# Moving the weight splits of the paged attention to other places inside an item

## The reference

```python
# L1_cond2, per sequence: 32 query heads, 8 key/value heads of 128 channels
q = einsum('bsd,ed->bse', x, Wq); k = einsum('bsd,ed->bse', x, Wk); v = einsum('bsd,ed->bse', x, Wv)
q, k = rope(rmsnorm(q)), rope(rmsnorm(k))
k_all = concat([k_cache[block_table], k]); v_all = concat([v_cache[block_table], v])   # 512 cached + 128 own keys
probs = softmax(where(valid, q @ k_all^T * SCALE, -1e30))
o = probs @ v_all
h = einsum('bse,de->bsd', o, Wo)
# L1_ffn: layernorm, int8-like fake-quantised linear, gelu, another such linear; added to x
```

## Time and profile before

| | us |
|---|---|
| median of 3 runs | 2129.42 (2124.53 to 2130.46) |
| the profiled execution: its own time | 2129.42 |
| the profiled execution: its span | 2127.6 |
| busy in the span: PE, PEld | 2030.9, 1714.6 |
| busy in the span: DVE, ACT, POOL | 1538.7, 1333.8, 812.6 |
| items of the paged attention | from 972.86 to the end of the span |

### The profile page before, as it was taken

One profiled execution on the slowest core, in us unless ns is written; L12 is line 12 of the kernel. 1 busy time (PEld: TensorE's weight loads), 2 busy tenths in 40 slices (PEclk: granted clock), 3 DMA queues, 4 the chain that ended last, 5 costly groups with the idle time before them and its releaser, 6 DMA issues.

```text
span 2127.6 us, 35433 instructions
## 1 busy us (share of the span) xinstructions
PE 2030.9 (95%) x12241; PEld 1714.6 (81%) x12264; DVE 1538.7 (72%) x3387; ACT 1333.8 (63%) x3810; POOL 812.6 (38%) x803
## 2 busy tenths in 40 slices
PE   6999977999999999989999999999999999999985
PEld 5777755888888888868888888888888888888863
DVE  5566753566566555557788888887878888888887
ACT  3566662455455445446677776777767767777785
POOL 4100001400000000005666666666666666666773
PEclk9999998999999999989999999999999999999997
DMA  8011101011011001101111121111111111112000
GB/s 295 26 51 46 51 1 69 5 56 65 31 35 65 30 26 50 55 13 67 31 60 52 32 82 31 62 51 33 61 50 46 67 32 62 51 31 82 28 31 30
DMA packets 45009, 108.65 MB, mean 51 GB/s; under 512 B 15634, under 2 KB 21010, under 8 KB 40354
## 3 DMA queue, kind: packets, MB, share of 16 engines
q1 hardware_dynamic: 28450, 72.80, 9.8%
q0 software_dynamic: 16384, 33.59, 5.2%
HBM read 103.20 MB, written 3.15 MB: 50 GB/s over the span
## 4 chain that ended last, share of the span: by engine, by line
PE 86%; DVE 8%; ACT 4%; issue 1%; DMA 0%; POOLq 0%; POOL 0%; SPq 0%; DVEq 0%; ACTq 0%
PE PS L1510 10%; PE PS L1414 8%; PE PS L1522 8%; PE PS L1276 8%; PE PS L1336 7%; PE PS L1477 7%; PE PS L1495 6%; PE PS L1428 4%; PE PS L1289 4%; PE PS L1480 3%; PE PS L344 3%; PE PS L1304 3%; PE PS L1321 2%; PE PS L488 2%; PE PS L334 2%
## 5 line engine op out<-in xcount | busy, mean ns | idle before, releaser
L2342 POOL DMA_INDIRECT kcache<-in_kcache,rows x256 | 250.9, 980 | 564.1 <-DVE x_res L1655 493.4
L2350 POOL DMA_INDIRECT vcache<-in_vcache,rows x256 | 257.5, 1006 | 139.9 <-PE PS L1304 64.2
L1816 DVE CUSTOM_DVE_ANT_0 pr<-PS,ffn_weights,sm 128x640 f32<-128x640 f32 x256 | 225.4, 885 | 96.4 <-PE PS L1480 96.4
L2195 ACT ACTIVATE pr<-pr,sm 128x640 f32<-128x640 f32 x256 | 212.5, 830 | 36.8 <-DVE sm L1816 36.1
L1832 DVE TENSOR_TENSOR prT_lo<-PS,prT_hi 128x512 fp32r<-128x512 f32 x320 | 209.0, 686 | 34.3 <-ACT prT_hi L2206 28.6
L2206 ACT ACTIVATE prT_hi<-PS 128x512 fp32r<-128x512 f32 x320 | 178.2, 597 | 60.8 <-PE PS L1495 60.3
L1495 PE MATMUL PS<-consts,pr 128*128 128x128 f32 x1280 | 172.9, 273 | 3.1 <-DVE prT_lo L1832 2.1
L1495 PEld LDWEIGHTS PS<-consts,pr 128*128 128x128 f32 x1280 | 149.8, 141 | 28.1 <-DVE prT_lo L1832 3.6
L2356 POOL TENSOR_TENSOR vcached_lo<-vcache,vcached_hi 128x512 fp32r<-128x512 f32 x64 | 83.3, 1301 | 223.7 <-ACT vcached_hi L2178 223.7
L2058 ACT ACTIVATE pr<-pr,sm 128x128 f32<-128x128 f32 x256 | 99.7, 391 | 105.6 <-DVE sm L1645 105.6
L1477 PE MATMUL PS<-kT_lo,qT_hi 128*128 128x320 f32 x512 | 154.1, 309 | 0.0
(11 more groups left out here) (322 smaller groups left out, 6359.3 us busy)
## 6 DMA issues: line engine op xcount, KB each, us to landing
arena<-in_wqkv SPq DMA_DIRECT2D x16, 1536.0 KB, 6.4
arena<-in_wo SPq DMA_DIRECT2D x16, 1024.0 KB, 5.4
arena<-in_wcT SPq DMA_DIRECT2D x8, 1024.0 KB, 5.7
kcache<-in_kcache,rows POOLq DMA_INDIRECT x256
vcache<-in_vcache,rows POOLq DMA_INDIRECT x256
arena<-in_xT SPq DMA_DIRECT2D x8, 256.0 KB, 6.2
x_res<-in_x SPq DMA_DIRECT2D x1, 2048.0 KB, 14.8
ffn_weights<-in_alibi SPq DMA_DIRECT2D x2, 1024.0 KB, 5.9
```

The source lines that it names most:

```text
L1816: dve.tensor_tensor_reduce(pr2[:, h, :].rearrange("p (a n) -> p a n", a=2), PS[:, SCORE_BANK[h]:SCORE_BANK[h] + 2, 0:HALF], keymask[:, b, ...
L2195: act.activation(pr2[:, h, :], pr2[:, h, :], ACT.Exp, bias=nm2[:, h:h + 1], scale=-1.0, accum_out=rs2[:, h:h + 1]).then_inc(a2_ex, 1)
L2342: pool.indirect_dma_start(out=kcache[:, c, :], out_offset=None, in_=T["kcache"], in_offset=bass.IndirectOffsetOnAxis(ap=rows[:, g, b, c:c ...
L2350: pool.indirect_dma_start(out=vcache[:, c, :], out_offset=None, in_=T["vcache"], in_offset=bass.IndirectOffsetOnAxis(ap=rows[:, g, b, c:c ...
```

## The change

On PE, the step with b = 6 no longer does parts 0 and 1 of the q projection ahead of `turn_q`; part 0 moves to where part 2 was and parts 1, 2, 3 to where part 3 was. On ACT and DVE, the splits of parts 0, 1 and 2 move out of the end of the step with b = 5 into the one with b = 6: parts 0 and 1 ahead of the split of q (on DVE ahead of `lo_of_q`), parts 2 and 3 ahead of chunk 3 of the probabilities, part 4 stays at the end. The splits of the output weights (b = 0) move too: heads 0 and 1 go ahead of chunk 2, heads 2 and 3 between the chunks 3 and 4. No instruction is added or removed. Lines below 1526 keep their numbers; later ones of DVE are one higher and those of ACT three higher.

```diff
--- before.py
+++ after.py
@@ -1524,6 +1524,7 @@
                 mm.then_inc(a2_out, 1)
 
             def step(i):
+                new_weights = i % B == B - 2
                 scores(i)
                 if i + 1 < ITEMS:
                     project_kv(i + 1)
@@ -1537,14 +1538,14 @@
                 turn_probs(i, 0)
                 turn_probs(i, 1)
                 more = i + 2 < ITEMS
-                if more:
+                if more and not new_weights:
                     project_q(i + 2, (0, 1))
                 if i + 1 < ITEMS:
                     turn_q(i + 1)
                 weigh(i, 0)
                 turn_probs(i, 2)
                 if more:
-                    project_q(i + 2, (2,))
+                    project_q(i + 2, (0,) if new_weights else (2,))
                 weigh(i, 1)
                 if i + 1 < ITEMS:
                     turn_k(i + 1)
@@ -1554,7 +1555,7 @@
                 if b >= 4:
                     turn_hidden(b - 4, 1, i)
                 if more:
-                    project_q(i + 2, (3,))
+                    project_q(i + 2, (1, 2, 3) if new_weights else (3,))
                 if b >= 2:
                     turn_hidden(b - 2, 0, i)
                 weigh(i, 2)
@@ -1880,31 +1881,33 @@
                     clamp(q - 4, 1)
                 if i:
                     add(i - 1)
+                if new_weights:
+                    lo_of_weights(g + 1, 0)
+                    lo_of_weights(g + 1, 1)
                 if more:
                     lo_of_q(i + 1)
-                lo_of_probs(i, 2)
                 if new_out:
                     lo_of_out_weights(g, 0)
-                if new_weights:
-                    lo_of_weights(g + 1, 3)
+                    lo_of_out_weights(g, 1)
+                lo_of_probs(i, 2)
                 if more:
                     lo_of_own_k(i + 1)
                 if q >= 2:
                     clamp(q - 2, 0)
                 if q >= 1:
                     variance(q - 1)
+                if new_weights:
+                    lo_of_weights(g + 1, 2)
+                    lo_of_weights(g + 1, 3)
                 lo_of_probs(i, 3)
+                if new_out:
+                    lo_of_out_weights(g, 2)
+                    lo_of_out_weights(g, 3)
                 if q >= 5:
                     add_hidden(q - 5)
                 lo_of_probs(i, 4)
-                if new_out:
-                    for h in range(1, GH):
-                        lo_of_out_weights(g, h)
                 if new_weights:
                     lo_of_weights(g + 1, 4)
-                if b == B - 3 and g < G - 1:
-                    for part in range(3):
-                        lo_of_weights(g + 1, part)
                 if q >= 1:
                     centre(q - 1)
                 if q >= 2:
@@ -2239,31 +2242,31 @@
                     hi_of_x(i + ITEMS - FROM_X)
                 hi_of_probs(i, 0)
                 hi_of_probs(i, 1)
+                if new_weights:
+                    hi_of_weights(g + 1, 0)
+                    hi_of_weights(g + 1, 1)
                 if more:
                     hi_of_q(i + 1)
                 if new_out:
                     hi_of_out_weights(g, 0)
+                    hi_of_out_weights(g, 1)
                 hi_of_probs(i, 2)
-                if new_out:
-                    hi_of_out_weights(g, 1)
-                if new_weights:
-                    hi_of_weights(g + 1, 3)
                 if more:
                     hi_of_own_k(i + 1)
                 if q >= 4:
                     to_bf16(q - 4, 1)
+                if new_weights:
+                    hi_of_weights(g + 1, 2)
+                    hi_of_weights(g + 1, 3)
                 hi_of_probs(i, 3)
+                if new_out:
+                    hi_of_out_weights(g, 2)
+                    hi_of_out_weights(g, 3)
                 if q >= 2:
                     to_bf16(q - 2, 0)
                 hi_of_probs(i, 4)
-                if new_out:
-                    hi_of_out_weights(g, 2)
-                    hi_of_out_weights(g, 3)
                 if new_weights:
                     hi_of_weights(g + 1, 4)
-                if b == B - 3 and g < G - 1:
-                    for part in range(3):
-                        hi_of_weights(g + 1, part)
                 if q >= 4:
                     hidden_copy(q - 4, 1, upto=NTH[q - 2, 0] + 1)
                 if q >= 2:
```

## The result

| | before | after |
|---|---|---|
| median (us) | 2129.94 of 4 runs (2124.53 to 2130.84) | 2157.82 of 4 runs (2150.94 to 2161.2) |
| the profiled execution: time, span | 2129.42, 2127.6 | 2157.68, 2155.9 |

The ratio is 1.0133, 95% interval 1.0113 to 1.0152: slower by 27.9 us, forecast 26.6. The time 2157.82 stands beside the forecast 2156.0. Two executions further down (2274.08 and 3216.71 us), whose mean granted clock was 0.84 and 0.61 instead of 0.98, are left out of all medians.

The account below looks back on a forecast made before the run. TensorE was taken as full, with VectorE nearly so in items with b = 6. Losses of 7 x 2.76 = 19.3 us (b = 6) and 7.3 us (b = 0) made 26.6 us, so 2156.0 us, range 2148 to 2168.

Parts of the forecast that it names:

- First wait: Items with b = 6: TensorE's first product after `turn_q` waits 0.94 us for VectorE's low part of chunk 0.
- Second wait: Items with b = 6: TensorE's q projection waits 1.66 us for VectorE's low part of weight part 0.
- Third wait: Items with b = 6: TensorE waits 0.25 us for VectorE's low part of weight part 2, behind ScalarE's high part.
- End of the step with b = 5: Three splits leave ScalarE's and VectorE's lists there; TensorE did not wait for them, so this gives 0.
- Output weights: Items with b = 0: moved output-weight splits cost 0.9 us an item, 7.3 us over eight items.
- the 0.05 for the two pieces between the chunks 3 and 4: Items with b = 0: chunk 4's low part stands behind two more output-weight pieces, put at 0.05 us.
- the transposes wait for chunk 2: Items with b = 0: TensorE's transpose of chunk 4 waits 0.87 us for VectorE's low part of chunk 2.
- The clock: New items with b = 6: a half-rate stretch could cost up to 1.7 us; not in the sum.
- (a): Rival: clock falls in nearly every item with b = 6, giving 38.5 us more, 2167.9 us; chance 0.14.
- (b): Rival: output weights in items with b = 0 are free, leaving 19.3 us alone, 2148.7 us; chance 0.10.
- (c): Rival: not slower, VectorE has the weight slice ready when TensorE asks, price 0, 2129.4 us; chance 0.04.
- the bounds 24 and 11: Upper bounds in us on the total loss: 24 for the items with b = 6, 11 for those with b = 0.

Follow-up runs that it names:

- e8: Changed kernel with VectorE's last two output-weight pieces behind chunk 4 and the first two still ahead of chunk 2; 2155.85 us on chip C, one run.
- e9: Changed kernel with VectorE doing chunk 2 first, then two output-weight pieces, the other two behind chunk 4; 2148.1 us on chip C, one run.
- e3: Kernel before with only TensorE's new order in items with b = 6, all weight splits left early; 2141.19 us, ratio 1.0032, chip B.
- e5: Changed kernel with weight parts 0 and 1 split at the end of the step with b = 5; 2148.23 us, ratio 1.0074 to the kernel before.
- e6: Changed kernel with VectorE's chunk 2 ahead of the first two output-weight pieces; 2157.16 us, ratio 1.0114 to the kernel before.
- after_again: The changed kernel, unaltered, profiled again on chip B; 2158.22 us (span 2156.4).
- e1: Changed kernel with the output weights split where they were before; 2148.68 us against 2134.82 for the kernel before, ratio 1.0074, chip B.
- e4: Kernel before, TensorE's order untouched, with weight parts 0, 1 and 2 split ahead of q in the item with b = 6; 2169.52 us, ratio 1.0173.
- e2: Kernel before with only the four output-weight pieces at their new places; 2141.09 us, ratio 1.0035, chip B.
- before_again: The kernel before, unaltered, profiled again on chip B; 2132.92 us (span 2131.1).
- g1: Kernel before with ScalarE's split of the next cached values moved ahead, into the step with b = 5; 2127.64 us against 2127.9, ratio 0.9997, chip C.
- g2: Kernel before with GpSimd writing the norm factors ahead of the next cached-value gathers in steps with b = 2; 2123.66 us, chip C, one run.

## Why the prediction was right

**The sum.** The items with b = 6 cost 21.7 us for 19.3 (20.3 without the fall of the clock in one of them), those with b = 0 8.8 for 7.3. Both are a little more than worked out, 3.9 together, and of that 2.6 don't show in the total, because the paged attention began 2.6 us earlier in this execution (970.24 for 972.86), with which the change has nothing to do: over the fourteen profiles it begins anywhere from 964.9 to 973.5. So it is partly luck that 27.9 measured stands so near 26.6.

The chips are a second piece of luck. It isn't known on which chips the first two profiles were taken. ScalarE's pick-up is 0.63 to 0.69 us in the one before, as on chip C, and 0.68 to 0.77 in the one after (item 0: 1.22), as on chip B, so the 27.9 may be a difference between two chips. On chip B, where both kernels were profiled again, the spans are 2131.1 and 2156.4: 25.3 us, of which 2.8 are two falls of the clock. The forecast of 26.6 is near either figure, but the items say that the same change costs less on chip B.

**The bound and the method.** TensorE full, VectorE next, ordinary items untouched: so it came out. VectorE's wait at the start of item 14 grew, as forecast, from 0.32 to 2.16 us. Laying out one item again from its own rows gave 19.93 us for item 14's kind (17.17 + 2.76). Chip C, whose pick-ups are those of the first profile, shows 19.97 to 19.99 in the items of e8 and e9 whose clock did not fall. On the chip of the profile after, ScalarE took up chunk 0 at 0.75 (1226.53 to 1227.28) instead of 0.64, and the item took 20.0 to 20.14.

**First wait**, 0.94: 0.93 measured. e3 shows that TensorE's order makes it with the splits left early. **Second wait**, 1.66: 1.73; e5, with the slices early, has none. **Third wait**, 0.25: 0.20 to 0.28, over the chain through ScalarE that the prediction named. Together with 0.08 more for the transposes they make 20.14. **End of the step with b = 5**, 0: right for the first profile and on chip C. On chip B it is wrong: there the splits at that place cost the kernel before 0.8 us an item, and taking them away gives that back, so the change costs 2.1 us an item there, not 2.9.

**Output weights**, 0.9 an item: 1.1 measured (18.27). The wait for chunk 2 was sized right (0.95 from start to start, 0.85 as the loss of e8). What was mis-sized is the 0.05 for the two pieces between the chunks 3 and 4: e8, without them, and the changed kernel lie 0.25 apart. Of that, 0.11 is there already when chunk 4 is transposed (14.87 us into the item for 14.76) and goes with the later pick-up; the other 0.14 is the two pieces. And "the transposes wait for chunk 2" was a real wait but not the only bound, as e6 shows: a reader who had moved VectorE's chunk 2 ahead on the strength of it, and nothing else, would have lost another 0.3 us.

**The clock.** The prediction left one or two items in its own range and gave (a) a chance of 0.14. One of seven fell (item 30, 21.44 us). Four stretches around it, columns as in the earlier trace rows:

```profile
1506.89:1510.30 3.41, 3.41 (x21) 2.86 (x20) 3.20 (x11) 2.54 (x6) 3.02 (x4) 1.00 0.20 60
1510.30:1513.72 3.42, 1.90 (x12) 1.25 (x10) 3.22 (x8) 2.95 (x6) 2.62 (x3) 1.00 0.06 19
1513.72:1517.13 3.41, 2.83 (x7) 2.18 (x8) 2.23 (x4) 0.00 (x0) 2.20 (x2) 0.58 0.20 60
1517.13:1520.54 3.41, 3.41 (x20) 2.81 (x19) 2.56 (x5) 3.10 (x6) 0.00 (x0) 0.92 0.02 5
```

After a stretch with TensorE busy for 1.90 of 3.42 us the mean granted clock of the next two was 0.58 and 0.92, together some 3.4 us at the lower level (1.2 GHz), and the item grew by 1.4, not by the 1.7 that the prediction gave as the most. Over the six profiles of kernels with these items (after, after_again, e1, e6, e8, e9) it fell in 8 of 42 items: 1, 2, 1, 0, 3 and 1. The length of the item's waits doesn't decide it: TensorE's two long ones have brackets of 0.62 and 1.48 in item 30, where it fell, and 0.68 and 1.48 in item 14, where it did not. What does is open; in e8 it was every second one, the items 14, 30 and 46. It fell in all seven where the wait was 4.00 us in one piece (e4). The rule of the Trainium skill that the prediction weighed ("TensorE: Matmul & The Clock Gate", "Why this matters for your kernels") warns only of idle gaps longer than any of these; to stay under them isn't enough here, where the longest single wait of item 14's kind is 1.73 us.

**The rivals.** (a) is the paragraph above: one item in the profile, not nearly all. (b) fell with e1 and e2: the output weights cost 8.8 us. (c) fell with the slot of part 0's low part: it began 1230.73, 4.20 us after the transposes; (c) needed it by 2.5. Its idea that freeing the end of the item before helps has something to it, though: on chip B it gives back 0.8 us, too little.

**One point that the prediction missed.** VectorE's work in item 14 is now 17.14 us, as much as a whole item of before lasts, and it has waits of its own besides (0.42 us ahead of the key at 1233.64 and 0.23 ahead of part 2). So even with every wait of TensorE covered by another order, this item could hardly have stayed at 17.17. That is an argument from the busy time; no run tried such an order.

**The range.** The bounds 24 and 11 give 2164.4, not the 2168 that the prediction names for them; the upper end of its range rests on (a) alone.

## What to carry to other kernels

When one engine is full and the next is nearly so, lay out one item again in the new order with the durations of its own rows, and go by the starts: that gave the waits here to within 0.1 us. Before you believe that a wait is *the* cost of an order, add up what the waiting chain's engine must do ahead of its last deadline; moving the one instruction that is late may only show the next bound. Splits for the next group cost nothing at the end of a step where nobody waits for them (0.8 us on chip B), and 2 to 3 us in all where they stand ahead of data that TensorE is waiting for. And compare kernels on one chip: the difference between two chips was as large as a fifth of this effect.

## What the runs showed that was not expected

The same kernel is not the same on two chips. On chip C, and in the first profile, ScalarE takes up chunk 0 at 0.63 to 0.65 us after the start of its transposes, in every item from the third to item 57. On chip B it takes 0.66 to 0.81, and 1.52 to 1.58 in the items with b = 6 of the kernel before, which makes them 17.95 instead of 17.17; seven times that is 5.5 us, and the kernel is 5 to 7 us slower there (2134.82 and 2133.22 for 2127.9). ScalarE's three splits at the end of the step before start later there, too: the first 1.43 us ahead of the item instead of 1.80, after a wait for TensorE's last reader of the old weights. With two splits there instead of three the pick-up is 1.06 to 1.11, with none it is 0.7.

The traces narrow the cause down. ScalarE isn't still busy with older work: the row at 1223.83 above shows it idle for 1.13 us just ahead of the late pick-up. On chip B the pick-up follows the end of GpSimd's last gather instruction for the cached values, by 0.88 to 1.15 us in every item from 2 to 56 of all its profiles, whether that gather ends early or late. Item 14's last gather in before_again, and then in the first profile:

```profile
1221.81 0.94 POOL L2350 DMA_INDIRECT vcache<-in_vcache,rows  x1 [0.30 <-issue]
```

```profile
1223.39 0.95 POOL L2350 DMA_INDIRECT vcache<-in_vcache,rows  x1 [0.31 <-issue]
```

From its end to the pick-up pass 1.08 us (1222.75 to 1223.83) and 0.52 (1224.34 to 1224.86); in g1 and g2 on chip C it is 1.9 us in item 14 of the one, while in item 10 of the other the gather ends after the pick-up. It isn't a wait for the last data, which the expectation of g2 takes it for: in item 14 of before_again packets of the gather still move after the pick-up (a share of the DMA engines of 0.06 from 1224.0 to 1224.2). That the pick-up comes with the gathers on chip B is shown, and that it comes from them is not; TensorE's signal may be late for a reason of its own. The two kernels built to tell this apart ran on the chip that doesn't show it.
